# Local projections: q and k from fp32r products, both rotated on VectorE, rests on GpSimd

## The reference, cut to what matters

```python
def _layer(x, wqkv, qs, ksc, wo, ...):
    h = shift_token(x)                    # second half of the features from the row before
    q, k, v = jnp.split(h @ wqkv, 3, axis=-1)
    q, k, v = (to_heads(q), to_heads(k), to_heads(v))      # 8 heads of 64
    q = l2norm(q) * qs
    k = l2norm(k) * ksc
    q, k = rotary_xpos(q, k)
    o = local_attention(q, k, v)
    x = x + o @ wo
    ...                                   # a feed-forward part follows
```

## Time and profile before

| what | value |
|---|---|
| median of 3 runs | 2657.73 us (2653.59 to 2662.21) |
| profiled execution | 2644.05 us |
| its span in the profile | 2642.3 us |
| mean granted TensorE clock, share of full | 0.932 |
| busy: PE, PEld, DVE, ACT, POOL (us) | 2326.9, 1721.0, 1251.5, 1054.8, 693.0 |
| projections, first layer | from about 549.7 to 682.4 us |
| projections, second layer | from about 975.4 to 1109.1 us |

### The profile page before, as it was taken

The page is one execution under the profiler, slowest core; times in us unless marked ns, Lnnn a source line. Parts: engine busy times, 40 slices in busy tenths (PEclk is TensorE's granted clock), DMA queues, the critical chain, the costliest instruction groups (busy, mean ns, idle before and its releaser), DMA issues. The chain is left out here.

```text
span 2642.3 us, 43456 instructions
## 1 busy us (share of the span) xinstructions
PE 2326.9 (88%) x13702; PEld 1721.0 (65%) x13703; DVE 1251.5 (47%) x2874; ACT 1054.8 (40%) x2555; POOL 693.0 (26%) x684
## 2 busy tenths in 40 slices
PE   7997497869998998899798998999999399979998
PEld 4665496634565774466586666569999156567887
DVE  4664200479766329866433664100000357547864
ACT  1563132324454523355522664114444036544332
POOL 1000201247321537611342000400000510045443
PEclk8997698889999999999899997999999699979999
DMA  8761242010000000000005751112221386200001
GB/s 186 155 152 67 80 163 87 23 40 0 25 0 15 25 16 0 24 0 0 15 1 107 134 103 69 58 44 104 105 103 36 95 151 129 42 27 24 20 24 38
DMA packets 110696, 164.20 MB, mean 62 GB/s; under 512 B 15257, under 2 KB 95114, under 8 KB 105578
## 3 DMA queue, kind: packets, MB, share of 16 engines
q1 hardware_dynamic: 101570, 140.55, 21.2%
q0 software_dynamic: 7680, 20.98, 2.5%
q10 hardware_dynamic: 1320, 1.03, 0.2%
HBM read 114.83 MB, written 47.32 MB: 61 GB/s over the span
## 5 line engine op out<-in xcount | busy, mean ns | idle before, releaser
L1017 DVE TENSOR_REDUCE xa_mx<-ps 128x2 f32<-128x512 f32 x384 | 247.2, 686 | 103.3 <-PE ps L669 101.6
L141 PE MATMUL ps<-ones 128*128 128x384 f32 (+1 forms) x414 | 158.8, 514 | 100.3 <-DMA ex_rows<-rows_out,rows_back 37.8
L876 ACT ACTIVATE xn_tok<-ps 128x512 f32<-128x512 f32 x384 | 210.5, 601 | 57.0 <-PE ps L677 51.2
L1447 PEld LDWEIGHTS ps<-ex_xT,ex_w 128*128 128x128 f32 x1792 | 212.0, 194 | 7.3 <-issue 4.5
L1447 PE MATMUL ps<-ex_xT,ex_w 128*128 128x128 f32 x1792 | 212.6, 278 | 3.9 <-issue 3.9
L1454 PE MATMUL ps<-ex_w,ex_h 128*128 128x256 f32 x896 | 202.7, 379 | 0.0
L669 PE MATMUL ps<-xa_ks,xa_qs 48*128 48x256 f32 (+1 forms) x768 | 158.1, 324 | 30.4 <-DMA xa_qs<-x_maxima 9.7
L2108 PE MATMUL ps<-lo_w,lp_hs 128*128 128x512 f32 x384 | 176.0, 609 | 4.7 <-ACT lp_hs L2156 2.8
L141 PEld LDWEIGHTS ps<-ones 128*128 128x128 f32 x414 | 85.7, 228 | 143.6 <-issue 52.5
L1454 PEld LDWEIGHTS ps<-ex_w,ex_h 128*128 128x128 f32 x896 | 165.9, 190 | 20.3
L669 PEld LDWEIGHTS ps<-xa_ks,xa_qs 48*128 48x128 f32 (+1 forms) x768 | 107.0, 193 | 104.7 <-DVE xa_mx L1017 52.1
(11 more groups left out here) (342 smaller groups left out, 5260.4 us busy)
## 6 DMA issues: line engine op xcount, KB each, us to landing
xa_ks<-x_keys SPq DMA_DIRECT2D x144, 128.0 KB
xa_qs<-x_queries SPq DMA_DIRECT2D x144, 128.0 KB, 4.7
ex_w<-in_L0f_w_dram SPq DMA_DIRECT2D x16, 1024.0 KB, 7.2
ex_w<-in_L2f_w_dram SPq DMA_DIRECT2D x16, 1024.0 KB, 6.7
x_keys<-xa_khl SPq DMA_DIRECT2D x24, 512.0 KB, 5.7
x_queries<-xa_qhl SPq DMA_DIRECT2D x24, 512.0 KB, 2.9
ex_stage<-rows_in POOLq DMA_DIRECT2D x64, 128.0 KB, 2.3
rows_out<-ex_rows SPq DMA_DIRECT2D x56, 128.0 KB, 1.7
```

Of the source, the lines that this page charges most:

```text
L141: self.nc.tensor.matmul(self.ps[:, bank, 0:wide * P], self.ones[:], self.ones[:].unsqueeze(1).to_broadcast([P, wide, P]), start=True, stop ...
L876: nc.scalar.activation(pT[:, h % SLOTS].rearrange("p k q -> p (k q)"), c.ps[:, S_BANK + (HEADS * b + n) % 3], ACT.Exp).then_inc(exped.sem, 1)
L1017: nc.vector.tensor_reduce(mx[:, half, :, col], c.ps[:, M_BANK + h % 2].rearrange("p (t n) -> p t n", t=2), AX_X, ALU.max).then_inc(max_put ...
L1447: ins = nc.tensor.matmul(c.ps[:, f % 4, 0:P], w1[:, buf, k, f * P:(f + 1) * P], xT[:, k], start=(k == 0), stop=(k == KD - 1))
```

## The change

- q and k are computed from three fp32r products in place of one fp32 product: every fp32 operand is split into a lead (its value rounded to fp32r) and a rest, and lead x lead, rest x lead and lead x rest are added. v stays fp32. A project is then 12 fp32r products and two fp32 ones.
- The weights' leads are cast by ScalarE (`lead_w`) and their rests subtracted by VectorE, once at the start of the block. The rows' leads are cast by ScalarE at the end of `put_rows`, and their rests subtracted by GpSimd (`rest`), once per sequence. TensorE waits for `h_rest` where it waited for `h_put`.
- VectorE rotates q and k together, with instructions twice as wide; GpSimd rotates nothing. `t2` is now for one tile, and `sq` lies in the other half of its space.
- ScalarE waits for the weights in TensorE's place; in front of its first project TensorE has four products of `keep_busy`.
- `wo` is fetched in `local_weighing`, after the mask has come and before w1. VectorE waits there for the mask alone, and TensorE waits for `wo` in `output`.

```diff
-        def rotate(engine, eng, step, tt, side):
+        def rotate(dve, step, tt):
-            a = t1[:, tt, side].rearrange("p (h d) -> p h d", h=LH)
-            b = t2[:, tt, side].rearrange("p (h d) -> p h d", h=LH)
+            a = t1[:, tt].rearrange("p a (h d) -> p a h d", h=LH)
+            b = t2.rearrange("p a (h d) -> p a h d", h=LH)
             for lo, hi in ((0, HALF), (HALF, LD)):
...
+            def rest(i):
+                pool.wait_ge(*h_lead(i + 1))
+                pool.wait_ge(*qkv_done(2 * i))
+                nc.gpsimd.tensor_tensor(hl[:], hs[:], hh[:].bitcast(F32), ALU.subtract).then_inc(h_rest.sem, 1)
             stage(0)
+            rest(0)
             with pool.Fori(0, B - 1) as i:
                 stage(i + 1)
-                rotate_k(i, 0)
-                rotate_k(i, 1)
+                rest(i + 1)
...
             def project(i, tt):
-                pe.wait_ge(*h_put(i + 1))
+                pe.wait_ge(*h_rest(i + 1))
...
-                for n in range(3):
-                    for k in range(KD):
+                for n in range(2):
+                    pe.wait_ge(*w_rest(n + 1))
+                    for a, (hp, wp) in enumerate(((hh, wh), (hl, wh), (hh, wl))):
+                        for k in range(KD):
+                            ins = nc.tensor.matmul(c.ps[:, 3 * tt + n, :], hp[:, k, tt * P:(tt + 1) * P],
+                                                   wp[:, k, n * INNER:(n + 1) * INNER],
+                                                   start=(a == 0 and k == 0), stop=(a == 2 and k == KD - 1))
+                for k in range(KD):
+                    ins = nc.tensor.matmul(c.ps[:, 3 * tt + 2, :], hs[:, k, tt * P:(tt + 1) * P],
+                                           wqkv[:, k, 2 * INNER:], start=(k == 0), stop=(k == KD - 1))
...
             turn_rows(0, h_put(0))
-            pe.wait_ge(*w_in(16))
+            c.keep_busy(4, 0)
             project(0, 0)
...
             def put_rows(i):
                 act.wait_ge(*h_turned(i + 1))
                 act.wait_ge(*qkv_done(2 * i))
+                act.wait_ge(*h_rest(i))
...
+                act.wait_ge(*pool_s(1))
+                act.wait_ge(*h_put(i + 1))
+                nc.scalar.copy(hh[:], hs[:]).then_inc(h_lead.sem, 1)
...
+            def lead_w(n):
+                cols = slice(n * INNER, (n + 1) * INNER)
+                nc.scalar.copy(wh[:, :, cols], wqkv[:, :, cols]).then_inc(w_lead.sem, 1)
+            act.wait_ge(*w_in(16))
+            lead_w(0)
             put_rows(0)
+            lead_w(1)
...
         def _(dve):
+            for n in range(2):
+                cols = slice(n * INNER, (n + 1) * INNER)
+                dve.wait_ge(*w_lead(n + 1))
+                nc.vector.tensor_tensor(wl[:, :, cols], wqkv[:, :, cols], wh[:, :, cols].bitcast(F32), ALU.subtract
+                                        ).then_inc(w_rest.sem, 1)
...
         def _(sp):
+            sp.wait_ge(*loaded(16))
+            sp.dma_start(wo[:], dram["L1f_wo"][d]).then_inc(loaded.sem, 16)
             sp.dma_start(w[:], dram["L1f_w1"][d]).then_inc(w_in.sem, 16)
...
             def output(i):
+                pe.wait_ge(*loaded(32))
                 pe.wait_ge(*o_put(2 * i + 2))
```

More of the change, by code:

```diff
@@ L2043, in local_projections @@
         zst, hs = sb("zst", [P, 2, D]), sb("hs", [P, KD, S])
-        sq, ss = sb("sq", [P, 2 * INNER]), sb("ss", [P, 2, 2 * LH])
+        (wh, wl), (hh, hl) = ([c.sb(f"lp_{n}_{part}", shape, F32R, ctx) for part in ("lead", "less")]
+                              for n, shape in (("w", [P, KD, 2 * INNER]), ("h", [P, KD, S])))
+        w_lead, w_rest, h_lead, h_rest = (c.sig(n) for n in ("w_lead_put", "w_rest_put", "h_lead_put", "h_rest_put"))
+        ss = sb("ss", [P, 2, 2 * LH])
         root, rn = sb("root", [P, 2, 2 * LH]), sb("rn", [P, 2, 2 * LH])
@@ L2053, in _ @@
             fetch(sp)
[L2055 to L2058 removed]
+        def rotate(dve, step, tt):
+            a = t1[:, tt].rearrange("p a (h d) -> p a h d", h=LH)
+            b = t2.rearrange("p a (h d) -> p a h d", h=LH)
             for lo, hi in ((0, HALF), (HALF, LD)):
[L2060 to L2066, removed]
+                src = a[:, :, :, HALF - lo:HALF - lo + HALF]
+                step.mark(nc.vector.tensor_tensor(
+                    b[:, :, :, lo:hi], src, tab[:, :, 1, tt, lo:hi].unsqueeze(2).to_broadcast([P, 2, LH, HALF]), ALU.mult))
+            step.settle(dve)
+            step.link(dve, nc.vector.tensor_tensor(
+                a, a, tab[:, :, 0, tt].unsqueeze(2).to_broadcast([P, 2, LH, LD]), ALU.mult))
+            return nc.vector.tensor_tensor(a, a, b, ALU.add)
         @block.gpsimd
@@ L2220, in _ @@
                     rot.n = SETUP + 3 * tt
-                    rotate(nc.vector, dve, rot, tt, 0).then_inc(q_rot.sem, 1)
+                    rotate(dve, rot, tt).then_inc(qk_rot.sem, 1)
     loaded.spent(32)
-    pool_s.spent(1 + 6 * B)
+    pool_s.spent(1)
+    for sgn in (w_lead, w_rest):
+        sgn.spent(2)
+    for sgn in (h_lead, h_rest):
+        sgn.spent(B)
     pair_s.spent(SETUP + 6 * B)
@@ L2464, in local_attention @@
         v = c.sb("la_v", [P, NT, INNER], ctx=ctx)
-        wo, mask = c.sb("la_wo", [P, INNER // P, D], ctx=ctx), c.sb("la_mask", [P, 3 * WIN], ctx=ctx)
+        mask = c.sb("la_mask", [P, 3 * WIN], ctx=ctx)
         def fetch(sp):
-            sp.dma_start(wo[:], c.dram["L1f_wo"][d]).then_inc(c.sig("output_weights_in").sem, 16)
             sp.dma_start(mask[:], c.dram["window"]).then_inc(c.sig("output_weights_in").sem, 16)
-        t1, t2 = (c.xT[:, k].rearrange("p (t a n) -> p t a n", t=2, a=2) for k in range(KD))
-        local_projections(c, d, z, qT, kT, v, t1, t2, w, w_in, fetch)
+        t1 = c.xT[:, 0].rearrange("p (t a n) -> p t a n", t=2, a=2)
+        t2, sq = c.xT[:, 1, 0:2 * INNER].rearrange("p (a n) -> p a n", a=2), c.xT[:, 1, 2 * INNER:4 * INNER]
+        local_projections(c, d, z, qT, kT, v, t1, t2, sq, w, w_in, fetch)
         w_in.spent(16)
-        local_weighing(c, d, z, zstats, qT, kT, v, wo, mask, w, w_in)
+        local_weighing(c, d, z, zstats, qT, kT, v, mask, w, w_in)
 def local_ff(c, d, z, zstats, w1, w1_in, last):
```

32 lines of the change are left out of this document (11 added, 21 removed).

## The result

| what | before | after |
|---|---|---|
| median of 20 executions each, taken side by side | 2653.31 us (2645.78 to 2662.23) | 2658.93 us (2653.33 to 2669.01) |
| profiled execution (its span) | 2644.05 us (2642.3) | 2666.28 us (2664.1) |
| mean granted TensorE clock | 0.932 | 0.926 |
| projections, both layers | 266.3 us | 275.4 us |
| VectorE waiting for the squares, whole span | 10.3 us, 2 times | 26.4 us, 14 times |

The ratio is **1.0025, interval 1.0014 to 1.0035**: 5.6 us by the medians, slower, and within the 0.3% that I called no change. The stage's length is counted from GpSimd's first copy into `zst` to the cast of the mask that opens the weighing, in the profiled execution.

What follows compares the result with a forecast made beforehand. VectorE was taken to bound the projections. Per layer +1.2 us for the slots with the subtraction's turns, +1.35 start and -1.4 end, twice: +2.3, to 3 with the clock, on 2657.7: 2661 us, range 2645 to 2678.

Steps and rivals of the forecast that it cites:

- VectorE sets the pace, TensorE's rate gives nothing: Projections: VectorE's slots fill the 14.84 us pair, TensorE needs 13.5, so a faster TensorE alone would give nothing.
- Slot of 7.05, pair of 14.1: VectorE's work per 128-row tile, with q and k rotated together: 7.05 us against 7.42, before any cost of the subtraction.
- Third rival: VectorE's rotation: the 1024-wide instructions cost more than alone, slots of 7.4, +10 us, 2671; chance 0.08.
- The subtraction's turn, 0.95 a pair, pair 15.05: GpSimd's subtraction delays VectorE's 1024-wide sum by 0.95 us in 7 pairs a layer; pair 15.05 against 14.84.
- square, copies and cast follow VectorE's slot at a fixed distance: ScalarE's chain ahead of the subtraction: moves with VectorE's slot, placing the subtraction in the rotation, 4.72 us after slot start.
- It gives nothing and costs nothing while VectorE covers it; the cover is 1.3 us: TensorE's loop from project to project: 13.7 us, under VectorE's 15.05 a pair, so no effect on the time.
- about 2.3 (its turn awaited): Sign of a right forecast: length of GpSimd's subtraction in us, against 1.29 alone.
- second rival: TensorE's clock falls in the idle 2.4 us before project, which takes 1.7 us longer; pair 16.0, 2674; chance 0.19.
- first rival: The subtraction runs beside VectorE's reduction and costs nothing: -5.6 us a layer, 2646 us; chance 0.14.
- Start, +1.35 a layer: Start of the stage: products of ones at half clock delay the first project, ScalarE squares at 560.8, not 559.46.
- End, -1.4 a layer: End of the stage: the last transposes no longer wait for GpSimd's rotation of k, -1.4 us per layer.
- Output weights, 0: Fetching the output weights in the next stage: TensorE's wait covered by more than 20 us, cost 0.

Runs made afterwards that it cites:

- e6: The kernel before with VectorE rotating q and k together, and GpSimd's copy of the next rows waiting for the first tile's rotation: ratio 0.9955, 2641.24 us.
- e3: The changed kernel with k rotated by GpSimd as before, so fp32r products without the new rotation: ratio 1.0168 to the kernel before, 2698.33 us.
- e1: The changed kernel with four products of ones on TensorE ahead of its wait for the rests, in every pair but the first: ratio 0.9999 to the kernel before.
- e4b: The changed kernel with GpSimd's subtraction waiting until the rotation is done, and three products of ones in TensorE's gap: ratio 0.9988 to the kernel before.
- e7: e1 without the four keep_busy products ahead of the stage's first project: ratio 1.0025 to the kernel before.
- e2: The kernel before with only the rotation changed, VectorE rotating q and k together, and q and k still fp32 products: ratio 0.9966.

## Why the prediction was right or wrong

The number, 2661 for 2658.93, was near, the ratio lies within 0.3%, and the range holds the result. That it is so near is luck. I set the change on a median of 2657.7 where the kernel before measures 2653.31 beside the changed one, 4.4 too high, and put the change at 3 us where it cost 5.6; the two errors offset each other. The mechanism was right only in part.

- **VectorE sets the pace, TensorE's rate gives nothing**: right for the kernel before. Taking 0.37 us a slot off VectorE gave 12 us (e6); faster products, without it, cost 1.7% (e3).
- **Slot of 7.05, pair of 14.1**: right, 14.14 (e6). Third rival (a dearer 1024-wide rotation): out, 1.225 mean.
- **The subtraction's turn, 0.95 a pair, pair 15.05**: right as a mechanism and in size when the clock is held: 15.09, the sum at 2.17, the subtraction asked for 4.88 us after the slot's start, where I had 4.72 (e1). In the changed kernel itself mostly not paid: 2 of 32 sums. In the pair shown, the slot starts at 576.12 and the subtraction at 582.25, 6.13 later, behind VectorE's sum: the turn is then GpSimd's and TensorE's to pay. My step "square, copies and cast follow VectorE's slot at a fixed distance" failed there, because ScalarE had come to wait for TensorE: 109.7 us over the run, against 38.8 with the gap filled.
- **"It gives nothing and costs nothing while VectorE covers it; the cover is 1.3 us"**: this is the step that failed, in two ways. First, TensorE's loop is 14.51 us at full clock and not 13.7 (from the end of one project, 612.46, to that of the second after it, 626.97). The loop's sum took the subtraction at 1.29, though the prediction's own signs said "about 2.3 (its turn awaited)"; it takes 1.69 here. And from its end to the project it is 0.34, not 0.06. 14.51 is more than VectorE's own 14.1 (e6), so once a late square has carried the subtraction off the rotation, TensorE sets the pair. Second, the clock fell in or behind the gap in 10 of 14 pairs, and in the steady pairs each fall adds 1.6 us or more. The second was my second rival, given 0.19: its 1.7 us for a project was right in size (1.6), as was its mark "VectorE waiting for the square". It came about in part: the first layer's mean pair is 15.6 and the second's 16.0, where the forecast had 15.05 and the rival 16.0. Its added price (13 us for turns on top) was wrong, since a late square carries the subtraction off the rotation: the two costs replace each other. Filling the gap takes the ratio from 1.0025 to 0.9999.
- **Why the clock survived before**: the gaps ahead of project there are 1.08 and 0.39 us in the same pass (rows below), and the clock of the steady stretch is 1.00. That they are short enough is the likely reason, and no run tested it. The first rival (a free subtraction, faster) needed the subtraction late without TensorE late; e4b makes that by hand and is 0.1% faster than before, its interval reaching 1.0000.

```profile
1063.88 0.66 PE L2098 MATMUL ps<-eye,lp_zst 128*128 128x128 f32 x4 [1.08 <-ACT la_kT L2172]
...
1065.36 0.65 PE L2123 MATMUL ps<-eye,xn_T 128*128 128x128 f32 x4 [0.39 <-ACT lp_hs L2156]
```

- **Start, +1.35 a layer**: not seen. The changed kernel's two executions take 11.49 and 9.94, 11.39 and 10.90 us, those of the kernel before 10.78 and 11.24, 11.74 and 10.28: means of 10.9 and 11.0, each with a spread wider than the term. It was mis-sized at the clock: I let the products of ones end at 556.3, but in the first layer the clock is full by then and project starts at 554.94, two fp32r products taking 0.62 from the third on. Without the products of ones the first project begins 4.77 us after the copy into `zst` and not 5.26, but its v part comes 9.22 after it and not 8.29 (e7 against e1).
- **End, -1.4 a layer**: right, -1.42 (9.34 against 10.76 from the last reduction to the cast of the mask). TensorE's first products of the next stage also run at full clock, 1.53 us for four, where four took 2.90.
- **Output weights, 0**: right. They land 3.6 us after issue in the weighing, and the first product that needs them is at 711.18, some 24 us later; no wait on them is recorded.

The sum for the stage, by parts: from first to last reduction +12.5 us (forecast +2.4), start -0.6 (+2.7), end -2.8 (-2.8): +9.1 in this execution and +1.6 in the next. What stays open: the 17 us by which two executions of the unaltered kernel before differ outside this stage; no run here isolates it. Open too is what decides in a single pair whether the clock falls: at 616.90 and at 631.41 the changed kernel's project comes after idle times of 2.13 and 2.14 us, and the clock holds the first time (1.00) and falls the second (0.79).

## What to carry to other kernels

Ask of each new wait on TensorE what the clock will do in the idle time it opens, and price the loop at the lower level too: here a cover of 1.3 us reckoned at full rate was gone with the first fall. Price an instruction that takes turns at its contended length in both chains, that of its own engine too. Before moving work between VectorE and GpSimd, lay both timelines side by side and place what remains on GpSimd beside instructions of VectorE that read one operand; here one wait made GpSimd's copy free (e6), and one its subtraction (e4b). And faster products on an engine that wasn't the bound were worth nothing, while the steps that prepare their operands were paid.

## What the runs showed that I had not expected

- An idle time of 1.9 to 2.7 us on TensorE ahead of each project was enough here for the clock to fall in 8 of 12 pairs, and in the second execution of the same kernel in 5 of 12; behind the 3.6 to 4.0 us in each layer's first pair it fell all four times. In the pair shown: 1.00 granted before, 0.55 behind, 0.91 over the stage. Eight product records of ones in the gap keep 1.00 (e1).
- The turns also catch VectorE's `TENSOR_SCALAR` of 128x16, which reads one SBUF operand: 0.17 us alone, 0.52 beside a copy of GpSimd's (e4b). The Trainium skill (SBUF — State Buffer, section Who interferes with whom) exempts one-operand instructions only outside the two-port modes, and counts `tensor_scalar` among the operations that can enter them. The trace agrees that it contends; no run here shows the mode itself.
- GpSimd gets in between two VectorE instructions that are issued back to back (1.29 to 1.71 for the pair in e2), and a turn of the copy costs about as much (0.35 to 0.42 a pair) as half a subtraction (0.80).
